# A new hand-written order of steps for a kernel that runs selective scan, layer norms and FFN of three rows at once

## The chip, the cores and the metric

One core of one Trainium2 chip runs the kernel. The metric is device time in microseconds (us), from the first to the last instruction of the slowest (here the only) core, median of the runs. TensorE is called PE, VectorE DVE, ScalarE ACT, GpSimd POOL, and SyncE, which here only issues transfers, SP.

## The reference, cut to what matters

Sixteen rows of 512 tokens x 256 features go through one layer: a selective-scan block (Mamba), a residual and a layer norm, then a gated FFN with two hidden layers, a residual and a layer norm.

```
xx, res = split(x @ in_w.T);  xx = silu(causal_conv4(xx))           # 512 channels
delta_r, B, C = split(xx @ xproj_w.T);  delta = softplus(delta_r @ dt_w.T + dt_b)
h[l] = exp(delta*A) * h[l-1] + delta*B*xx     # 16 states per channel
y = sum_n h*C + xx*D;   y = (y * silu(res)) @ out_w.T
x1 = layernorm(x + y)
h = silu(x1 @ w1 * s1) * (x1 @ w2 * s2);  h = gelu(h @ h1 * s);  h = gelu(h @ h2 * s)
out = layernorm(x1 + h @ w3 * s)
```

## The kernel before

The program works on one row (512 tokens) per iteration, but on several rows at once: in `iteration(i)` the row `scan` = i is scanned, `front` = i+1 is prepared for its scan, `tail` = i-1 is gated, projected, normalised and starts its FFN, and `end` = i-2 finishes its FFN. i runs from -1 to 17. Iteration 0 has no tail, 1 no end; 15 has no front, 16 no scan; so 13 iterations (2 to 14) have all four.

An iteration has 64 steps, s = 0 to 63. All five engines walk through the same steps, each in its own strict order, and wait on semaphores for each other's data. A step is thus no moment in time but a place in each queue. Tables of constants say in which step a piece stands: the name tells the piece, the n-th number the step of its n-th instance. A number over 63 means step s-64 of the next iteration, where the same row is `end`.

The scan of a row is 32 pairs p (16 states x 4 blocks of 128 channels, two blocks a pair). For pair p:
- PE: `b_pair` transposes delta\*B\*u of the pair into PSUM, 8 transposes, called T(p) below. PSUM holds two pairs, so T(p) waits for pair p-2: for DVE's product with C (L800), or for the scan itself where the product is on POOL.
- DVE, step 2p: `scan_pair` (L789). Step 2p+1: `c_pair` (L800), C(p) below, except for the pairs in `POOL_PAIRS`, whose scan writes to `hC` in SBUF and whose product POOL makes (L983).
- ACT makes dA by Exp (`EXP_COUNT` says how many in each step) and dB by Copy with a scale.
- POOL, step 2p+1: a DMA adds the product into y (L991). `hC` has three slots.

Before the change T(p) stands in step 2(p-1), first of that step: T(1) in 0, T(21) in 40, T(31) in 60, and T(0) of the next row in 62.

The FFN matmuls are in 32 halves, h(0) to h(31) (`HALF_AT`, `half_tile`), each of 8 matmuls of 512 columns. Odd halves close an output tile: ACT applies Gelu (`GELU_AT`, L716), POOL splits it in a high and a low part (`SPLIT_AT`, L1028 and L1030), which the next layer needs. Then W(0) to W(3) (`E_W3`, `w3_tile`, 16 matmuls of 256 columns), and on DVE E_SCALE, E_ADD, E_STATS, E_NORM. The first FFN layer is `L1_AT` (PE, ACT Tanh, DVE L905 and L912) with `L1_SPLIT_AT` on POOL.

The tail: RES(c) (`T_RES`, PE) feeds ACT's tanh and DVE's gate (`T_GATE`, L884), POOL multiplies it in (step after), then OUT(t) (`T_OUT`, PE), T_ADD, T_STATS, T_NORM, and X1T (`T_X1T`).

The front: XX(c) (`F_XX`, PE), three conv taps on DVE (L815), tanh, product u (L821); then in step 39 DBL (`F_DBL`, PE L463), which needs all four u; in step 40 (`F_DBL_OUT`) ACT copies its result to `xdbl` (L669); DT(c) (`F_DT`, PE L478) reads xdbl and feeds the softplus: Abs, Relu, Exp on ACT, BASE on POOL (`F_BASE`, L999), PLUS and LOST on DVE (`F_PLUS` L835, `F_LOST` L841), four Ln on ACT in step 52, DELTA (L847) and DELTA_U (L852) on DVE in step 53. BT (`F_BT`, PE) makes the B columns; DU (`F_DU`) transposes delta\*u.

`xdbl` is a part of the tile `out_st`, which also holds the finished output of the row `end` until it is stored. So ACT waits for that store before it writes xdbl:

```
if s == F_DBL_OUT:
    act.wait_ge(pe_dbl, r + 1)
    if end is not None:
        act.wait_ge(out_stored, end * 16 + 16)
    nc.scalar.activation(xdbl, misc_ps[0:DTC + STATES, :], ACT.Copy)
```

The store is issued by SP in step `OUT_AT`. SP's queue is in step order too: before the store come the weight loads into the four-slot `ring` of all earlier steps, and the load that reuses the slot of h(m) stands in the step of h(m) and waits until PE has finished h(m) (`load_weights`, L358).

Of the kernel before, what the change touches and what calls it, by code (L numbers as in the profile page):

```python
# [19 lines left out]
TILES = STATES * DC  # L20
PAIRS = TILES // 2
# [16 lines left out]
QUARTERS = 2 * W3_SLOTS  # L38


T_RES = (0, 4, 5, 8)
T_GATE = (2, 5, 7, 11)
T_OUT = (12, 13, 14, 17)
T_ADD = (15, 18)
T_STATS = (17, 18)
T_NORM = 19
T_X1T = (20, 21)
E_W3 = (10, 11, 13, 14)
E_SCALE = (12, 17)
E_ADD = (14, 19)  # L50
E_STATS = (15, 21)
E_NORM = 22
L1_AT = (22, 23, 24, 25, 26, 27, 28, 29)
L1_SPLIT_AT = (22, 24, 25, 27, 28, 29, 30, 31)
HALF_AT = (31, 32, 34, 35, 36, 38, 40, 41, 42, 43, 45, 46, 47, 48, 49, 50, 51, 52, 53, 54, 55, 57, 59, 60, 62,
           63, 64, 65, 66, 68, 69, 71)
GELU_AT = (38, 39, 39, 46, 46, 47, 50, 51, 55, 57, 57, 65, 66, 67, 71, 71)
SPLIT_AT = (40, 42, 43, 48, 48, 49, 51, 52, 59, 59, 61, 66, 66, 67, 72, 73)
F_XX = (30, 32, 34, 36)
FIRST_XX = (30, 31, 32, 33)  # L60
F_DBL = 39
F_DBL_OUT = 40
F_BT = 46
F_BT_OUT = 51
F_DT = (40, 41, 43, 44)
F_PLUS = (45, 46, 48, 50)
F_BASE = (40, 41, 43, 46)
F_LOST = (46, 49, 51, 52)
F_LN = 52
F_DELTA = (53, 53, 53, 53)  # L70
F_DELTA_U = (53, 53, 53, 53)
F_Y = (55, 55, 58, 63)
F_DU = (54, 55, 56, 58)
F_XR = 51
SCALE_LEAD = 7

EXP_LEAD, DA_RING = 4, 8
EXP_COUNT = (1, 2, 0, 0, 3, 0, 3, 0, 0, 1, 0, 0, 0, 2, 1, 1, 2, 2, 0, 0, 3, 1, 1, 0, 1, 1, 2, 1, 2, 1, 0, 1, 1,  # L80
             0, 1, 1, 2, 2, 1, 0, 2, 1, 0, 1, 2, 2, 0, 0, 2, 2, 0, 0, 0, 2, 2, 2, 0, 0, 1, 1, 0, 1, 1, 2)
EXP_FIRST = EXP_LEAD
EXP_AT = [(EXP_FIRST + sum(EXP_COUNT[:s]), EXP_COUNT[s]) for s in range(TILES)]
PREP_AT = (-30, -27, -25, -24, -20, -12, -7, -5, -3, 2, 5, 12, 16, 17, 18, 20, 23, 26, 30, 33, 38, 39)
# [1 line left out]
FLAG_AT = 48  # L86
DVE_SLOTS = 12
X_FRONT_AT = 22
OUT_AT = 24
X32 = 4  # L90
RAW = 4
HC_SLOTS = 3
POOL_PAIRS = (0, 8, 12, 13, 16, 17)
FIRST_POOL_PAIRS = (0, 3, 4, 9, 14, 16, 17, 18, 25, 27, 28)


# [10 lines left out]
def build(nc, x, xT_in, in_wT, chan, xproj_wT, dt_wT, out_wT, ffn_w, ffn_s, w3_s, ident_in, out):  # L107
# [3 lines left out]
    with ExitStack() as ctx:  # L111
# [172 lines left out]
        def _(sp):  # L284
# [42 lines left out]
            def entry_step(e, full):  # L327

                used = e - (FULL_RING if full else RING)
                if used < 0:  # L330
                    return E_W3[-1]
                if used < FIRST_HALF:
                    return L1_AT[used]
                if used < FIRST_W3:
                    return HALF_AT[used - FIRST_HALF]
                return TILES + E_W3[(used - FIRST_W3) // QUARTERS]

# [77 lines left out]
        def _(pe):  # L415
# [14 lines left out]
            def b_pair(r, p):  # L430
                n, half = divmod(p, 2)
                if half == 0:
                    pe.wait_ge(dB_ready, r * (STATES * TT) + (n + 1) * TT)
                g = r * PAIRS + p - 2
                if g >= 0 and on_pool(g // PAIRS, g % PAIRS):
                    pe.wait_ge(scan_done, g + 1)
                elif g >= 0:
                    wait_product(pe, *divmod(g, PAIRS))
                for k in range(2):
                    c = 2 * half + k  # L440
                    transposes(scan_ps[:, 2 * (p % 2) + k], lambda t: dB[:, n % 2, t, c * P:(c + 1) * P], TT
                               ).then_inc(pe_dBu, 1)
# [46 lines left out]
            def tail_step(r, par, s):  # L489
                if s in T_RES:  # L490
                    c = T_RES.index(s)
                    if c:
# [7 lines left out]
                    in_proj(misc_ps, DC + c, xT_tail).then_inc(pe_res, 1)  # L500
                if s in T_OUT:
                    t = T_OUT.index(s)
                    if t == 0:
# [85 lines left out]
            def iteration(i, par, full):  # L589
                (scan, _), (front, fpar), (tail, tpar), (end, _) = rows(i, par)  # L590
                for s in range(TILES):
                    if s % 2 == 0:
                        if s // 2 + 1 < PAIRS:
                            if scan is not None:
                                b_pair(scan, s // 2 + 1)
                        elif front is not None:
                            b_pair(front, 0)
                    if i == 0 and s == FLAG_AT + 1:
                        pe.wait_ge(low_summed, 1)
                        nc.tensor.matmul(ffn_ps[0][0:1, 0:1], low_sum[:], ones[:], start=True, stop=True  # L600
                                         ).then_inc(low_total, 1)
                    if end is not None and s in E_W3:
                        w3_tile(end, E_W3.index(s), full)
                    if tail is not None:
                        tail_step(tail, tpar, s)
                    if front is not None:
                        front_step(i, front, fpar, s, tail)
                    if end is not None:
                        if s + TILES in HALF_AT:
                            half_tile(end, HALF_AT.index(s + TILES), full)  # L610
                    if tail is not None:
                        if s in L1_AT:
                            l1_tile(tail, L1_AT.index(s), full)
                        if s in HALF_AT:
                            half_tile(tail, HALF_AT.index(s), full)

# [12 lines left out]
        def _(act):  # L629
# [71 lines left out]
            def tail_step(r, s):  # L701
                if s in T_GATE:
                    c = T_GATE.index(s)
                    act.wait_ge(pe_res, r * DC + (c + 1))
# [52 lines left out]
        def _(dve):  # L757
# [216 lines left out]
        def _(pool):  # L974
# [65 lines left out]
            def iteration(i, par):  # L1040
                (scan, spar), (front, fpar), (tail, tpar), (end, _) = rows(i, par)
                for s in range(TILES):
                    if scan is not None and s % 2:
                        y_pair(scan, spar, s // 2)
                    if tail is not None:
                        if s - 1 in T_GATE:
                            gate_tile(tail, tpar, T_GATE.index(s - 1))
                        if s == T_STATS[-1]:
                            rstd_of(0, tail)
                        ffn_step(tail, s)  # L1050
                    if end is not None:
                        if s == E_STATS[-1]:
                            rstd_of(1, end)
# [62 lines left out]
```

## Time and profile before

| | |
|---|---|
| median of 3 runs | 2786.72 us (2784.66 to 2788.4) |
| profiled execution, its own time | 2779.47 us |
| its span | 2777.7 us |
| PE / DVE / ACT / POOL busy | 88% / 87% / 76% / 59% |
| mean granted PE clock | 0.944 |
| DMA | 209 GB/s mean |

Busy time is a share of the span. Idle time "until" a releaser is time in which an engine stood still until the named instruction of another engine had finished; it is printed in brackets behind an instruction, or summed over a window.

### The profile page before, as it was taken

How to read it: one execution, taken by the hardware profiler on the slowest of the kernel's cores; microseconds unless marked ns; L12 is line 12 of the kernel's file. 1: busy time of each engine (PE TensorE's matmuls, PEld its weight loads, DVE VectorE, ACT ScalarE, POOL GpSimd, SP SyncE). 2: the span in 40 equal slices, each digit the busy share in tenths (PEclk: the TensorE clock that was granted, in tenths of full speed). 3: DMA queues.
4: the chain of work that ended last, by engine and by line, in shares of the span. 5: the costliest groups of instructions: out<-in, count | busy, mean ns of one | idle time of the engine just before them, and what ended most of it. 6: DMA issues, size and time to landing. Idle time of an engine off the chain costs nothing. (4 is left out here: it accounts for less than half of the span.)

```text
span 2777.7 us, 36139 instructions
## 1 busy us (share of the span) xinstructions
PE 2439.1 (88%) x12034; PEld 1849.5 (67%) x12034; DVE 2418.8 (87%) x2386; ACT 2117.6 (76%) x3225; POOL 1635.3 (59%) x1577
## 2 busy tenths in 40 slices
PE   4467998989899898989989899998989999898988
PEld 2345676766767676676757677675766767676767
DVE  6789899999999989999998999999898999989730
ACT  5676887969788796978879697887969789696711
POOL 1345656665665666566556656655665675666644
PEclk7568999999999999999999999999999999999999
DMA  5988898989889898998989889898988889898933
GB/s 168 310 201 192 204 225 195 235 198 222 212 206 228 192 237 200 217 215 206 225 191 239 204 214 211 208 223 200 234 209 208 211 209 224 204 229 203 251 98 118
DMA packets 226798, 581.68 MB, mean 209 GB/s; under 512 B 25920, under 2 KB 26304, under 8 KB 226128
## 3 DMA queue, kind: packets, MB, share of 16 engines
q0 software_dynamic: 73728, 268.47, 52.3%
q1 hardware_dynamic: 152880, 310.84, 33.4%
q8 instruction: 99, 1.62, 0.2%
q14 instruction: 91, 0.75, 0.1%
HBM read 301.86 MB, written 20.45 MB: 116 GB/s over the span
## 5 line engine op out<-in xcount | busy, mean ns | idle before, releaser
L789 DVE TENSOR_TENSOR_SCAN scan_ps<-dA,scan_ps 128x1024 f32<-128x1024 f32 x411 | 939.8, 2287 | 121.6 <-PE scan_ps L421 116.5
L991 POOL DMA_DIRECT2D y<-hC x512 | 449.6, 878 | 676.2 <-DVE hC L800 513.7
L648 ACT ACTIVATE dB<-duT,bT 128x512 f32<-128x512 f32 x1024 | 715.4, 711 | 119.5 <-PE scan_ps L421 119.5
L421 PE MATMUL scan_ps<-ident,dB 128*128 128x128 f32 x4096 | 580.4, 288 | 147.5 <-DVE hC L800 121.3
L639 ACT ACTIVATE dA<-delta,a_neg 128x512 f32<-128x512 f32 (+1 forms) x1024 | 692.4, 711 | 1.1
L534 PE MATMUL ffn_ps<-hb_hi,ring 128*128 128x512 f32 x1536 | 652.4, 425 | 35.8 <-POOL hb_lo L1030 20.7
L421 PEld LDWEIGHTS scan_ps<-ident,dB 128*128 128x128 f32 x4096 | 501.6, 148 | 264.2 <-DVE hC L800 100.9
L534 PE MATMUL ffn_ps<-hb_lo,ring 128*128 128x512 f32 x1536 | 609.1, 397 | 0.0
L800 DVE TENSOR_TENSOR hC<-scan_ps,c_rows_sb 128x1024 f32<-128x1024 f32 x411 | 500.6, 1218 | 41.6 <-DMA y<-hC 9.7
L534 PE MATMUL ffn_ps<-ha_hi,ring 128*128 128x512 f32 x1024 | 437.9, 428 | 6.5 <-POOL ha_lo L1030 4.6
L534 PE MATMUL ffn_ps<-ha_lo,ring 128*128 128x512 f32 x1024 | 403.0, 394 | 0.0
L534 PEld LDWEIGHTS ffn_ps<-hb_hi,ring 128*128 128x128 f32 x1536 | 294.4, 192 | 130.3 <-DVE gate L905 36.5
L1030 POOL TENSOR_TENSOR ha_lo<-x,ha_hi 128x512 fp32r<-128x512 f32 x256 | 328.7, 1284 | 21.2
L534 PEld LDWEIGHTS ffn_ps<-hb_lo,ring 128*128 128x128 f32 x1536 | 295.2, 192 | 64.5 <-issue 10.8
L983 POOL TENSOR_TENSOR hC<-hC,c_rows_sb 128x1024 f32<-128x1024 f32 x101 | 253.1, 2506 | 122.4 <-DVE hC L789 120.6
L534 PEld LDWEIGHTS ffn_ps<-ha_hi,ring 128*128 128x128 f32 x1024 | 193.5, 189 | 99.3 <-issue 52.5
L1028 POOL CAST ha_hi<-x 128x512 fp32r<-128x512 f32 x256 | 204.5, 799 | 84.0 <-DVE x L912 69.4
L716 ACT ACTIVATE x<-ffn_ps,fs 128x512 f32<-128x512 f32 x256 | 172.8, 687 | 104.8 <-PE ffn_ps L534 102.6
L789 DVE TENSOR_TENSOR_SCAN hC<-dA,scan_ps 128x1024 f32<-128x1024 f32 x101 | 229.9, 2277 | 13.9 <-DMA y<-hC 10.1
L534 PEld LDWEIGHTS ffn_ps<-ha_lo,ring 128*128 128x128 f32 x1024 | 193.9, 189 | 48.1 <-issue 12.9
L1030 POOL TENSOR_TENSOR hb_lo<-x,hb_hi 128x512 fp32r<-128x512 f32 x128 | 167.9, 1312 | 10.6
L725 ACT ACTIVATE gate<-ffn_ps,s_half 128x512 f32<-128x512 f32 x128 | 88.3, 690 | 103.2 <-PE ffn_ps L534 103.2
(99 smaller groups left out, 3154.5 us busy)
## 6 DMA issues: line engine op xcount, KB each, us to landing
y<-hC POOLq DMA_DIRECT2D x512, 512.0 KB, 5.9
ring<-rounded_weights SPq DMA_DIRECT2D x704, 256.0 KB, 4.1
c_rows_sb<-c_rows SPq DMA_DIRECT2D x256, 256.0 KB, 4.7
x<-ffn_w SPq DMA_DIRECT2D x22, 512.0 KB, 7.7
rounded_weights<-ffn_w SPq DMA_DIRECT2D x22, 512.0 KB, 9.2
xt<-x_chan SPq DMA_DIRECT2D x16, 512.0 KB, 3.8
xt<-x_tok SPq DMA_DIRECT2D x16, 512.0 KB, 4.7
out_st<-x_chan SPq DMA_DIRECT2D x16, 512.0 KB, 4.2
```

Source lines behind the costliest of these rows:

```text
L421: mm = nc.tensor.transpose(dst[:, j * P:(j + 1) * P], src(j), ident[:])
L534: mm = nc.tensor.matmul(dst, w, a, start=(first and n == 0), stop=(last and n == len(steps) - 1))
L639: nc.scalar.activation(dA[:, s % DA_RING, s % 2:], delta2[:, par, c, s % 2:], ACT.Exp, scale=a_neg[:, c, n:n + 1]).then_inc(dA_ready, 1)
L648: nc.scalar.activation(dB[:, n % 2, t, :], duT[:, t, :], ACT.Copy, scale=bT2[:, par, t, n:n + 1]).then_inc(dB_ready, 1)
L716: nc.scalar.activation(x32[:, i % X32, :], ffn_ps[(2 * HC + i) % 3][:], ACT.Gelu, scale=fs[:, 2 + i // HC, i % HC:i % HC + 1]).then_inc(ge ...
L725: nc.scalar.activation(gate[:, o % 2, :], ffn_ps[2 * o % 3][:], ACT.Tanh, scale=s1_half[:, o:o + 1]).then_inc(l1_tanh, 1)
L789: nc.vector.tensor_tensor_scan(states, dA[:, a:a + 2, :].rearrange("p a l -> p (a l)"), b, 0.0, ALU.mult, ALU.add).then_inc(scan_done, 1)
L800: nc.vector.tensor_tensor(hC[:, (r * PAIRS + p) % HC_SLOTS], scan_ps[:, h:h + 2, :], c_rows[:, n % 2].unsqueeze(1).to_broadcast([P, 2, SEQ ...
L983: nc.gpsimd.tensor_tensor(hC[:, slot], hC[:, slot], c_rows[:, n % 2].unsqueeze(1).to_broadcast([P, 2, SEQ]), ALU.mult).then_inc(hC_pool, 1)
L991: pool.dma_start(y2[:, par, c:c + 2, :], hC[:, slot], accum_op=ALU.add).then_inc(y_added[p % 2], 16)
L1028: nc.gpsimd.tensor_copy(hi[:, i % HC, :], x32[:, i % X32, :]).then_inc(ffn_hi, 1)
L1030: nc.gpsimd.tensor_tensor(lo[:, i % HC, :], x32[:, i % X32, :], hi[:, i % HC, :].bitcast(F32), ALU.subtract).then_inc(ffn_lo, 1)
```

## The change

Only the order changes; no instruction is added or removed, and the number of pairs on POOL stays at six of 32.
- T(p) gets a table of its own, `B_AT`. Most of it equals the old rule; T(26) goes from step 50 to 51, T(31) from 60 to 61.
- Halves: h(5) 38 to 37, h(6) 40 to 38, h(7) 41 to 40, h(10) 45 to 44, h(11) 46 to 45, several of h(21) to h(25) one or two steps earlier, h(24) 62 to 61, and the last ones later: h(28) 66 to 67, h(30) 69 to 71, h(31) 71 to 72.
- DT(3) 44 to 45; BT 46 to 48; PLUS from 45, 46, 48, 50 to 43, 44, 47, 49; LOST, BASE and the splits beside them.
- The tail and end pieces of steps 0 to 21 are laid out anew: RES, W, OUT, E_SCALE.
- The store of the output, `OUT_AT`, goes from step 24 to 39.
- POOL's pairs: 0 and 13 are replaced by 2 and 11.

```diff
-T_RES = (0, 4, 5, 8)
-T_GATE = (2, 5, 7, 11)
-T_OUT = (12, 13, 14, 17)
+T_RES = (1, 5, 7, 9)
+T_GATE = (3, 5, 7, 11)
+T_OUT = (13, 14, 16, 17)
-T_STATS = (17, 18)
+T_STATS = (16, 18)
-E_W3 = (10, 11, 13, 14)
-E_SCALE = (12, 17)
-E_ADD = (14, 19)
-E_STATS = (15, 21)
+E_W3 = (11, 12, 15, 16)
+E_SCALE = (14, 18)
+E_ADD = (15, 19)
+E_STATS = (16, 21)
-L1_AT = (22, 23, 24, 25, 26, 27, 28, 29)
-L1_SPLIT_AT = (22, 24, 25, 27, 28, 29, 30, 31)
-HALF_AT = (31, 32, 34, 35, 36, 38, 40, 41, 42, 43, 45, 46, 47, 48, 49, 50, 51, 52, 53, 54, 55, 57, 59, 60, 62,
-           63, 64, 65, 66, 68, 69, 71)
-GELU_AT = (38, 39, 39, 46, 46, 47, 50, 51, 55, 57, 57, 65, 66, 67, 71, 71)
-SPLIT_AT = (40, 42, 43, 48, 48, 49, 51, 52, 59, 59, 61, 66, 66, 67, 72, 73)
+B_AT = (-2, 0, 2, 4, 6, 8, 10, 12, 14, 16, 18, 20, 22, 24, 26, 28, 30, 32, 34, 36, 38, 40, 42, 44, 46, 48, 51, 52,
+        54, 56, 58, 61)
+L1_AT = (22, 23, 25, 26, 27, 28, 29, 31)
+L1_SPLIT_AT = (22, 23, 24, 25, 27, 29, 30, 31)
+HALF_AT = (31, 32, 34, 35, 36, 37, 38, 40, 42, 43, 44, 45, 47, 48, 49, 50, 51, 52, 53, 54, 55, 56, 57, 59, 61, 62,
+           63, 65, 67, 69, 71, 72)
+GELU_AT = (38, 38, 39, 46, 46, 46, 49, 51, 55, 56, 57, 65, 66, 66, 71, 72)
+SPLIT_AT = (39, 41, 42, 47, 47, 49, 51, 51, 59, 60, 61, 65, 66, 68, 71, 71)
-F_BT = 46
-F_BT_OUT = 51
-F_DT = (40, 41, 43, 44)
-F_PLUS = (45, 46, 48, 50)
-F_BASE = (40, 41, 43, 46)
-F_LOST = (46, 49, 51, 52)
+F_BT = 48
+F_BT_OUT = 50
+F_DT = (40, 41, 43, 45)
+F_PLUS = (43, 44, 47, 49)
+F_BASE = (41, 45, 46, 50)
+F_LOST = (44, 47, 51, 53)
-F_Y = (55, 55, 58, 63)
-F_DU = (54, 55, 56, 58)
+F_Y = (56, 58, 58, 63)
+F_DU = (54, 56, 57, 59)
...
-OUT_AT = 24
+OUT_AT = 39
-POOL_PAIRS = (0, 8, 12, 13, 16, 17)
+POOL_PAIRS = (2, 8, 11, 12, 16, 17)
...
                 for s in range(TILES):
-                    if s % 2 == 0:
-                        if s // 2 + 1 < PAIRS:
-                            if scan is not None:
-                                b_pair(scan, s // 2 + 1)
-                        elif front is not None:
-                            b_pair(front, 0)
+                    if scan is not None and s in B_AT:
+                        b_pair(scan, B_AT.index(s))
+                    if front is not None and s - TILES in B_AT:
+                        b_pair(front, B_AT.index(s - TILES))
```

`EXP_COUNT` is rewritten too: the running count of Exp instructions differs from the old one by at most one in any step, and their total is the same.

## Rows read from the trace of the kernel before

**Rows 1.** DVE's DELTA_U groups, first and last of 13 (start us, duration us).
```profile
509.66 2.48 DVE L852 TENSOR_TENSOR du<-y,delta 128x512 f32<-128x512 f32 x4
...
2465.50 2.48 DVE L852 TENSOR_TENSOR du<-y,delta 128x512 f32<-128x512 f32 x4
```

**Rows 2.** Busy time in one period: PE, PEld, DVE, ACT, POOL, PEclk, DMA.
```profile
1327.09:1490.07 162.98, 148.95 (x754) 113.04 (x752) 150.71 (x149) 132.54 (x202) 101.34 (x98) 0.98 0.89 213
```

**Rows 3.** What DVE waited for in that period: us in total, times, longest.
```profile
DVE scan_ps L789 <- PE scan_ps L421: 7.3, 5, 3.4
DVE gate L884 <- ACT gate L707: 2.1, 3, 1.3
DVE delta L847 <- ACT out_st L688: 0.2, 1, 0.2
```

**Rows 4.** DVE timeline: scans 27, 7 (E_ADD behind it), 9.
```profile
1327.09 2.28 DVE L789 TENSOR_TENSOR_SCAN scan_ps<-dA,scan_ps 128x1024 f32<-128x1024 f32 x1
...
1377.16 2.28 DVE L789 TENSOR_TENSOR_SCAN scan_ps<-dA,scan_ps 128x1024 f32<-128x1024 f32 x1
1379.36 0.67 DVE L927 TENSOR_TENSOR out_st<-out_st,x 128x512 f32<-128x512 f32 x1
...
1386.49 2.30 DVE L789 TENSOR_TENSOR_SCAN scan_ps<-dA,scan_ps 128x1024 f32<-128x1024 f32 x1 [0.64 <-PE scan_ps L421]
```

**Rows 5.** DVE timeline: scan 22, C(22), scans 23 and 26, LOST, DELTA, scan 27.
```profile
1459.73 2.29 DVE L789 TENSOR_TENSOR_SCAN scan_ps<-dA,scan_ps 128x1024 f32<-128x1024 f32 x1 [3.41 <-PE scan_ps L421]
1462.15 1.22 DVE L800 TENSOR_TENSOR hC<-scan_ps,c_rows_sb 128x1024 f32<-128x1024 f32 x1
...
1465.52 2.29 DVE L789 TENSOR_TENSOR_SCAN scan_ps<-dA,scan_ps 128x1024 f32<-128x1024 f32 x1 [1.81 <-PE scan_ps L421]
...
1479.93 2.28 DVE L789 TENSOR_TENSOR_SCAN scan_ps<-dA,scan_ps 128x1024 f32<-128x1024 f32 x1
1482.13 1.45 DVE L841 SCALAR_TENSOR_TENSOR delta<-out_st,delta 128x512 f32<-128x512 f32 x1
...
1484.89 1.05 DVE L847 TENSOR_TENSOR delta<-out_st,delta 128x512 f32<-128x512 f32 x1 [0.19 <-ACT out_st L688]
...
1490.07 2.28 DVE L789 TENSOR_TENSOR_SCAN scan_ps<-dA,scan_ps 128x1024 f32<-128x1024 f32 x1
```

**Rows 6.** PE timeline, stretch between two rows' scans: T(0), T(8), T(9).
```profile
1342.49 1.06 PE L421 MATMUL scan_ps<-ident,dB 128*128 128x128 f32 x8 [0.69 <-DVE hC L800]
...
1380.83 1.04 PE L421 MATMUL scan_ps<-ident,dB 128*128 128x128 f32 x8
...
1385.35 1.04 PE L421 MATMUL scan_ps<-ident,dB 128*128 128x128 f32 x8
```

**Rows 7.** PE timeline of the softplus stretch: DBL, T(21), T(25), T(26).
```profile
1447.90 3.63 PE L463 MATMUL misc_ps<-y,xprojw 128*48 128x512 f32 x8 [1.45 <-DVE y L821]
1451.47 1.09 PE L421 MATMUL scan_ps<-ident,dB 128*128 128x128 f32 x8
...
1474.08 1.03 PE L421 MATMUL scan_ps<-ident,dB 128*128 128x128 f32 x8
...
1478.60 1.03 PE L421 MATMUL scan_ps<-ident,dB 128*128 128x128 f32 x8
```

**Rows 8.** ACT timeline: the copy to xdbl.
```profile
1451.57 0.59 ACT L669 ACTIVATE out_st<-misc_ps 48x512 f32<-48x512 f32 x1
```

**Rows 9.** SP timeline: ring load behind h(6), and the output store of that row.
```profile
1408.63 1.14 SPq L381 DMA_DIRECT2D out_tok<-out_st  x1
...
1455.68 0.32 SPq L358 DMA_DIRECT2D ring<-rounded_weights  x1
```

**Rows 10.** All 16 output stores, issue to landing.
```profile
DMA to landing us min/median/max: 2.6/5.0/6.7
```

**Rows 11.** POOL's accumulating transfers, issue to landing (last column, median).
```profile
y<-hC POOLq DMA_DIRECT2D x512, 512.0 KB, 5.9
```

**Rows 12.** POOL timeline: a split beside LOST and DELTA.
```profile
1481.73 1.29 POOL L1030 TENSOR_TENSOR hb_lo<-x,hb_hi 128x512 fp32r<-128x512 f32 x1
...
1484.12 1.27 POOL L1030 TENSOR_TENSOR hb_lo<-x,hb_hi 128x512 fp32r<-128x512 f32 x1
```

More of the change, by code:

```diff
@@ L79 @@
 EXP_LEAD, DA_RING = 4, 8
-EXP_COUNT = (1, 2, 0, 0, 3, 0, 3, 0, 0, 1, 0, 0, 0, 2, 1, 1, 2, 2, 0, 0, 3, 1, 1, 0, 1, 1, 2, 1, 2, 1, 0, 1, 1,
-             0, 1, 1, 2, 2, 1, 0, 2, 1, 0, 1, 2, 2, 0, 0, 2, 2, 0, 0, 0, 2, 2, 2, 0, 0, 1, 1, 0, 1, 1, 2)
+EXP_COUNT = (1, 2, 0, 0, 2, 0, 4, 0, 0, 1, 0, 0, 1, 2, 0, 2, 0, 3, 0, 0, 3, 0, 1, 1, 2, 0, 2, 0, 2, 2, 1, 0, 1, 1,
+             0, 0, 3, 2, 1, 0, 2, 1, 1, 1, 1, 1, 0, 0, 3, 2, 0, 0, 0, 2, 3, 1, 0, 0, 0, 1, 0, 2, 1, 2)
 EXP_FIRST = EXP_LEAD
```

## The prediction

> **What bounds the kernel now.** Start with what repeats. The 13 DELTA_U groups from 509.66 to 2465.50 us are 12 periods of 162.99 us [rows 1]: one row of the batch costs 163 us, and whatever the change does, it does 13 times. Then the busy time in one period: DVE works 150.7 of 162.98 us, PE 149.0 [rows 2]. Two engines are within 2 us of each other, so neither is "the" bound: the reader has to ask of each stretch which of the two is waited for.
>
> The waits of DVE give that. In a period it stands still 7.3 us for transposes, 2.1 us for ACT's gate tanh and 0.2 us for a Ln, together 9.6 us [rows 3]; the rest of its 12.3 idle us are the small gaps between instructions. That 9.6 us is the most an order of steps can win where it adds no gap: 13 x 9.6 = 125 us.
>
> Now the two timelines, side by side. They fall into four legs.
> - Leg 1, from T(0) at 1342.49 to T(9) at 1385.35 [rows 6], is paced by PE: scan 9 starts 0.64 us late on T(9) [rows 4]. DVE's waits of this leg are all of rows 3 except the 3.41 and 1.81 us of scans 22 and 23 and the Ln: 7.3 - 3.41 - 1.81 + 2.1 = 4.2 us [rows 3, 5].
> - Leg 2, from scan 9 at 1386.49 to DBL at 1447.90, is paced by DVE: it has no DVE wait, and PE waits 1.45 us for the last u before DBL [rows 4, 7].
> - Leg 3, from DBL to T(26) at 1478.60, is PE's: 30.7 us without a stop [rows 7], while DVE waits 3.41 and 1.81 us [rows 5].
> - Leg 4, from scan 26 at 1479.93 to C(30) and the next T(0), is DVE's again: T(0) waits 0.69 us for C(30) [rows 5, 6].
>
> The path runs PE, DVE, PE, DVE. A wait inside a PE leg is won only if PE has less to do before the last transpose of that leg.
>
> **The change, leg by leg.**
>
> *Leg 1.* Before, T(0) to T(9) had between them h(24) and all of h(25) to h(31), RES, W(0) to W(3), OUT(0) to OUT(2). After, h(24) stands in front of T(0), and W(3) and OUT(2) behind T(9) (same step, after it). A half costs 1.8 us: T(25) to T(26) is 4.52 us with two halves and a transpose group of some 0.9 [rows 7]. W(3) with OUT(2) is the distance T(8) to T(9), 4.52 less 0.9 = 3.6 us [rows 6]. So PE reaches T(9) up to 5.4 us sooner; DVE needed it 4.2 us sooner at most, and PE stops being the pace. I follow DVE through steps 62 to 20 in the new order and find one wait left, about 0.5 us, for the tanh of gate 1: RES(1) stands behind h(28), T(3). The order also costs something. Where nothing stands between a scan and its own C, C starts 2.42 us after the scan [rows 5]; with a filler in the even step the filler starts after 2.20 [rows 4]. In steps 2 and 12 the fillers (gate 0, E_SCALE 0) go to odd or pool steps, the new pool pair 2 takes one of these gaps away: net about 0.2 us. Leg 1: -4.2 + 0.5 + 0.2 = -3.5 us. What is hidden in front of T(0) is h(24): PE waited 0.69 us there [rows 6], and in front of T(26) to T(29) a split and the DU chain leave it another 1 to 2 us.
>
> *Leg 2.* DVE's instructions are the same; L1 tiles and pool pairs trade places (step 22 loses a gap, 24 gains one). The price of the moves is 0. PE gets l1(7) behind XX(0), so h(1) will wait some 2 us for the last split; XX(2) waits for conv taps anyway, so this is cover that PE's idle time pays. Leg 2: 0.
>
> *Leg 3.* Between DBL and T(26) stood nine halves, h(6) to h(14), four DT and BT. After: h(7) to h(15), four DT and BT, five transpose groups in both. PE's 30.7 us stay. Nearly all waits that scans 22 and 23 lose come back at scans 24 and 26. What does change is the entry. The store of the output now stands in SP's step 39, behind the ring load that waits for the end of h(6) in step 38. h(6) will end just as u is ready, that is when DBL starts. SP then issues the load (0.32 us) and the store, about 0.5 us after h(6) [rows 9]; stores land 5.0 us (2.6 to 6.7) after their issue [rows 10]. ACT may write xdbl 5.5 us after h(6), where before it did so 3.67 us after DBL began [rows 7, 8]. DT(0) reads xdbl, and PE's queue stands behind it. If h(6) ends 0.2 us before DBL, leg 3 grows by 5.5 - 3.67 - 0.2 = 1.6 us; by the extremes of the landing, 0 to 3.3 us. Steady-state stores landed near 5, so I take 1.6. The old place had 43 us of cover (1408.63 to 1451.57) [rows 8, 9].
>
> *Leg 4.* Before, scan 26 to scan 27 took 10.14 us [rows 5]. LOST(3) in it lasted 1.45 us and the first DELTA 1.05, both with a POOL split running [rows 5, 12], where their uncontended kin take 0.68. After, h(15) stands in front of T(26) and both last splits in step 51: POOL is through with them before LOST(3), about 1.1 us. The Ln of three channels no longer stands behind LOST(3), 0.2 us. Scan 26 had 0.2 us of slack to T(26), now none, 0.2. Leg 4: -1.5 us.
>
> The cause of those long instructions is also a rule: the Trainium skill, SBUF — State Buffer, section Who interferes with whom, says that a VectorE instruction with two SBUF inputs, or in a two-port mode, and a GpSimd instruction that reads SBUF exclude each other for their whole length. The trace agrees: 1.45 against 0.68 us.
>
> Sum per full period: -3.5 + 0 + 1.6 - 1.5 = **-3.4 us**, 162.98 to about 159.6. Over 13 periods: -44 us. Iteration 15 has no front but leg 1: -3.5. Iteration 1 has no end, so no leg 1 and no store: about -1. The start (iterations -1, 0) and the end (16, 17, PE alone, same matmuls): 0. Total -48.5. The profiled execution would go from 2779.5 to about 2731; the median of the runs lies 7.2 us above that execution, so 2786.7 - 48.5 = 2738.
>
> **The rivals.**
> - *The store is hidden* (chance 0.18): h(6) ends 2 us before the last u, or the store lands in 3 us. Then a period gains 5.0, the total is 13 x 5.0 + 4.5 = 70: 2717 us. Against it: landings [rows 10].
> - *Half of it lost to new waits* (0.20): T_ADD(1) needs OUT(3), which PE reaches at nearly the same moment; or the store lands after 6.7 us. A period gains 1.2 to 2: 2760 to 2770 us.
> - *The lock moves instead of going* (0.05): by the rule above PLUS, LOST, DELTA, DELTA_U and Y, 20 instructions, can each be caught by a split. A catch costs about 0.75 us [rows 5, 12]; four more of them outside DVE's waits than now take 3 of the 3.4 us. About 2782. For it: BASE and the splits move beside PLUS and LOST; against: in leg 3 DVE waits anyway.
> - *Slower: POOL blocks* (0.13). Split 15 stands in POOL's step 7, its Gelu in ACT's step 8, behind h(31). POOL stands there, behind it gate 2 and the transfers y(4) and y(5). C(7) needs the `hC` slot of y(4), which lands 5.9 us after its issue [rows 11]. By my walk y(4) lands some 1 us before C(7) wants it. If POOL is later by x > 1 us, DVE waits x - 1, and T(9), W(3), OUT(3) with it. From x = 4.4 us on the period is longer than before; at 6 us it is 1.6 us longer: about 2808. Against it: POOL is the idlest of the four [rows 2].
> - The forecast itself: 0.44.
>
> **How the numbers follow.** Less than 0.2% either way (5.6 us) is about what a measurement of this kernel can tell from no change. Faster: 0.44 + 0.18 + 0.20 = 0.82, of which 0.01 is taken for misses; same: the lock rival and the edge of the others, 0.07; slower 0.12. The likeliest case alone spans 2725 to 2752 (store 0 to 3.3 us a period gives the sides). The 8-in-10 range reaches from the hidden store, 2712, to the upper end of the lost half and a little more, 2778.
>
> **What the profile of the changed kernel would show.** Right: periods of 159 to 160 us; no wait of scan 9 on T(9) and less than 1 us on gates; the store issued within 1 us of the end of h(6); ACT's L669 waiting for out_tok and PE idle before DT(0) for 1 to 2 us; LOST(3) at 0.7 us. Wrong: L669 without a wait (hidden store); DVE waiting for y<-hC at C(7) (slower rival); T_ADD(1) waiting for OUT(3); more L841 and L847 above 1 us.

## The result and the profile after

The changed kernel takes 2839.72 us (median of 4 runs, 2823.25 to 2846.12) beside 2786.23 for the one before: ratio 1.0187, 95% interval 1.0151 to 1.0223. I forecast 2738. It is slower by 1.9%, and its runs differ more among themselves than those of before do.

The profiled execution took 2834.73 us, its span is 2832.9. DELTA_U again marks the periods (start, duration), to be held against [rows 1]:

```profile
514.64 2.49 DVE L852 TENSOR_TENSOR du<-y,delta 128x512 f32<-128x512 f32 x4
...
2518.20 2.49 DVE L852 TENSOR_TENSOR du<-y,delta 128x512 f32<-128x512 f32 x4
```

(2518.20 - 514.64) / 12 = 167.0 us a period, before 163.0. All 13 periods together grew by 50.2 us, start and end by 2.5 us each; that is the whole difference of the spans, 55.2. The periods are no longer equal, either: 164.8 to 171.3 us. Two of them, and one more from the middle (length, PE, PEld, DVE, ACT, POOL busy, granted clock, DMA share, GB/s; compare [rows 2]):

```profile
514.64:680.27 165.63, 149.22 (x754) 113.64 (x753) 148.67 (x149) 132.02 (x202) 101.18 (x98) 0.98 0.87 210
...
680.27:849.13 168.86, 154.53 (x754) 117.68 (x753) 149.02 (x149) 131.99 (x202) 100.64 (x98) 0.94 0.86 206
...
1349.43:1516.62 167.19, 152.69 (x754) 117.07 (x753) 149.56 (x149) 131.87 (x202) 100.71 (x98) 0.95 0.87 208
```

DVE's work did not grow; it waits more. The clock of PE, 0.98 before, differs from period to period. It is a mean over two levels, 1.2 and 2.4 GHz (granted 0.5 and 1.0): before, 8.4 us of each period passed at the lower one, in one place, around a stop of PE of 2.8 us; now it is 12.9 us on average, in other places too. DVE's waits over two periods (1352.3 to 1685.5; us, times, longest; [rows 3] are for one):

```profile
DVE scan_ps L789 <- PE scan_ps L423: 13.2, 10, 1.9
DVE gate L884 <- ACT gate L707: 5.5, 6, 1.5
DVE xt L891 <- PE misc_ps L510: 3.7, 2, 1.9
DVE y L815 <- ACT y L656: 2.4, 3, 1.7
DVE xt L891 <- PE ffn_ps L510: 2.4, 2, 1.2
```

The first two groups are those of before: 6.6 instead of 7.3 us a period for transposes, 2.8 instead of 2.1 for gates. The next three are new: T_ADD(0), the conv taps that stand behind XX(2), T_ADD(1). PE's timeline of the first place says why:

```profile
1394.94 0.28 PE L536 MATMUL ffn_ps<-ring,ha_lo 128*128 128x256 f32 x1
1397.71 0.35 PE L536 MATMUL ffn_ps<-ring,ha_hi 128*128 128x256 f32 x1 [2.49 <-DMA ring<-rounded_weights]
...
1398.26 1.89 PE L423 MATMUL scan_ps<-ident,dB 128*128 128x128 f32 x8
```

W(0) stands still for 2.49 us in front of its last quarter, for weights whose load SP issued when h(31) was done:

```profile
1391.24 0.32 SPq L360 DMA_DIRECT2D ring<-rounded_weights  x1
```

It landed 6.3 us later. W(0) itself began 2.3 us after that issue. In the kernel before it began 3.2 us after it, and the load landed after 4.2 us (mean of 13 periods); W(0)'s last quarter, 1.6 us behind its first, had 0.6 us to spare. In the changed kernel the means are 2.3 and 6.3 us. The load and W(0) of before, then W(0) of the changed kernel:

```profile
1366.95 0.32 SPq L358 DMA_DIRECT2D ring<-rounded_weights  x1
```

```profile
1370.14 0.36 PE L534 MATMUL ffn_ps<-ring,ha_hi 128*128 128x256 f32 x1
```

```profile
1393.55 0.36 PE L536 MATMUL ffn_ps<-ring,ha_hi 128*128 128x256 f32 x1
```

So the order takes 0.9 us away, as T(5) now stands in front of h(31) and no longer between h(31) and W(0), and the landing takes 2.1 us longer: 0.9 + 2.1 - 0.6 = 2.4 us, the mean stop. Which transfers lengthen it no run separates in full: POOL's pairs and Exp alone, on another base, make it 4.7 us instead of 4.0 (b_softplus_pairs_exp beside b_new_softplus).

The transposes behind the stop take 1.89 us instead of 1.03 [rows 6, 7]: the clock has fallen. The second place is h(1), which waits for POOL's split of the last tile of the first FFN layer:

```profile
1458.70 0.50 PE L536 MATMUL ffn_ps<-ha_hi,ring 128*128 128x512 f32 x1 [2.14 <-POOL ha_lo L1030]
...
1461.49 1.83 PE L423 MATMUL scan_ps<-ident,dB 128*128 128x128 f32 x8
```

The clock falls again, XX(2) comes late, and DVE waits for its conv base:

```profile
1465.89 2.32 DVE L815 SCALAR_TENSOR_TENSOR y<-misc_ps,conv_half,y 128x511 f32<-128x511 f32 x3 [1.69 <-ACT y L656]
```

Third, the store of the output, with ACT's copy to xdbl and PE's DT(0) behind it, where before ACT wrote xdbl at once [rows 8]. SP, ACT, PE:

```profile
1478.04 0.43 SPq L383 DMA_DIRECT2D out_tok<-out_st  x1
```

```profile
1482.21 0.59 ACT L669 ACTIVATE out_st<-misc_ps 48x512 f32<-48x512 f32 x1 [1.34 <-DMA out_tok<-out_st]
```

```profile
1477.58 3.63 PE L465 MATMUL misc_ps<-y,xprojw 128*48 128x512 f32 x8
1481.14 1.09 PE L423 MATMUL scan_ps<-ident,dB 128*128 128x128 f32 x8
1482.86 1.12 PE L480 MATMUL misc_ps<-out_st,dtw 16*128 16x512 f32 x2 [0.62 <-ACT out_st L669]
```

Fourth, the end of the softplus stretch on DVE, as forecast against [rows 5]: LOST(3) and DELTA at 0.68 us, scan 26 to scan 27 in 8.99 us.

```profile
1510.04 2.29 DVE L789 TENSOR_TENSOR_SCAN scan_ps<-dA,scan_ps 128x1024 f32<-128x1024 f32 x1 [1.59 <-PE scan_ps L423]
...
1513.61 0.68 DVE L841 SCALAR_TENSOR_TENSOR delta<-out_st,delta 128x512 f32<-128x512 f32 x1
1514.21 0.69 DVE L847 TENSOR_TENSOR delta<-out_st,delta 128x512 f32<-128x512 f32 x1
...
1519.03 2.29 DVE L789 TENSOR_TENSOR_SCAN scan_ps<-dA,scan_ps 128x1024 f32<-128x1024 f32 x1
```

The starts of the 32 scans on DVE cut a period into stretches that every run can be compared by. The means over the 13 full periods, in us, worked out from the DVE timelines of the profiled executions, with the median of the runs in the last column:

| run | s27-s0 | s0-s9 | s9-s10 | s10-s15 | s15-s19 | s19-s26 | s26-s27 | period | median |
|---|---|---|---|---|---|---|---|---|---|
| before | 19.82 | 39.59 | 7.07 | 28.95 | 22.46 | 34.92 | 10.17 | 162.98 | 2786 |
| after | 19.52 | 39.36 | 8.92 | 27.98 | 25.11 | 36.97 | 8.99 | 166.84 | 2840 |
| a_h31_early | 19.59 | 38.54 | 7.95 | 27.60 | 25.51 | 36.51 | 8.98 | 164.69 | 2802 |
| a_old_tail_end | 19.54 | 39.66 | 7.06 | 27.75 | 24.88 | 37.78 | 8.99 | 165.66 | 2809 |
| a_old_l1 | 19.58 | 38.90 | 8.92 | 29.35 | 22.47 | 37.31 | 8.98 | 165.51 | 2812 |
| a_out24 | 19.58 | 39.61 | 8.91 | 28.01 | 25.35 | 35.00 | 8.99 | 165.46 | 2818 |
| a_w3_load_cut | 19.58 | 38.01 | 8.68 | 27.85 | 25.06 | 36.61 | 8.99 | 164.78 | 2814 |
| a_w1_load_cut | 19.57 | 39.75 | 8.92 | 27.93 | 24.93 | 36.25 | 8.99 | 166.33 | 2831 |
| a_h31_l1_out24 | 19.57 | 38.29 | 7.78 | 29.52 | 22.55 | 35.00 | 8.99 | 161.70 | 2767 |
| r_h29_behind_res1 | 19.57 | 38.22 | 7.85 | 29.48 | 22.55 | 35.01 | 8.98 | 161.68 | 2768 |
| r_pe_relieved | 19.58 | 36.86 | 8.61 | 29.62 | 22.58 | 35.01 | 8.99 | 161.25 | 2750 |
| r_act_relieved | 19.57 | 38.27 | 7.88 | 29.40 | 22.78 | 35.01 | 8.99 | 161.90 | 2765 |
| r_both_relieved | 19.62 | 36.72 | 8.64 | 29.37 | 22.64 | 35.01 | 8.98 | 160.99 | 2749 |
| b_new_softplus | 19.54 | 39.63 | 7.06 | 29.06 | 22.46 | 35.01 | 8.99 | 161.73 | 2761 |
| b_softplus_out39 | 19.56 | 39.58 | 7.06 | 28.95 | 22.45 | 36.94 | 8.99 | 163.53 | 2792 |
| b_softplus_pairs_exp | 19.56 | 39.72 | 7.06 | 29.19 | 22.50 | 35.01 | 8.99 | 162.01 | 2771 |
| b_softplus_old_b | 19.55 | 39.59 | 7.06 | 28.95 | 22.44 | 33.33 | 9.93 | 160.86 | 2751 |
| b_out39 | 19.81 | 39.68 | 7.06 | 28.95 | 22.45 | 35.29 | 10.19 | 163.43 | 2789 |
| r_old_b_pairs_exp | 19.58 | 38.38 | 7.77 | 28.95 | 22.46 | 33.33 | 9.93 | 160.39 | 2742 |

Leg 1 of the prediction is s0-s9; E_SCALE(1) moved from in front of scan 9 to behind it (0.6 us), so s0-s10 is the fair sum: 46.66 before, 48.28 after. Leg 2 is s10-s19, leg 3 s19-s26, leg 4 s26-s0. Medians carry some 0.2% (the intervals of the ratios are 0.15 to 0.35% to each side); the stretches are steadier, where a run's periods are equal.

### The profile page after: what moved, and what is told of

The parts are those of the page before. It is cut to its first block and busy times, and to the rows that moved or that the text cites. A ratio compares the mean times of both kernels' runs of the same rounds, so it can differ in the third digit from the quotient of the medians.

```text
span 2832.9 us, 36139 instructions
## 1 busy us (share of the span) xinstructions
PE 2469.8 (87%) x12034; PEld 1877.1 (66%) x12034; DVE 2404.5 (85%) x2386; ACT 2109.0 (74%) x3225; POOL 1623.3 (57%) x1577
## 5 line engine op out<-in xcount | busy, mean ns | idle before, releaser
L423 PE MATMUL scan_ps<-ident,dB 128*128 128x128 f32 x4096 | 589.7, 292 | 139.3 <-DVE hC L800 99.5
L536 PE MATMUL ffn_ps<-hb_hi,ring 128*128 128x512 f32 x1536 | 660.6, 430 | 34.3 <-POOL hb_lo L1030 18.4
L423 PEld LDWEIGHTS scan_ps<-ident,dB 128*128 128x128 f32 x4096 | 510.6, 150 | 261.6 <-issue 101.3
L536 PE MATMUL ffn_ps<-ha_lo,ring 128*128 128x512 f32 x1024 | 409.6, 400 | 0.0
L536 PE MATMUL ffn_ps<-ring,ha_hi 128*128 128x256 f32 x512 | 140.0, 308 | 35.9 <-DMA ring<-rounded_weights 33.7
```

The costliest lines, as they stand in the source:

```text
L423: mm = nc.tensor.transpose(dst[:, j * P:(j + 1) * P], src(j), ident[:])
L536: mm = nc.tensor.matmul(dst, w, a, start=(first and n == 0), stop=(last and n == len(steps) - 1))
```

## The experiments

**One piece of the change undone at a time.** First h(31) and its neighbours.

```diff
-HALF_AT = (..., 65, 67, 69, 71, 72)
+HALF_AT = (..., 65, 66, 68, 69, 71)
-GELU_AT = (..., 66, 71, 72)
+GELU_AT = (..., 66, 71, 71)
```

> The changed kernel with the last four FFN halves of a row back in their old steps: h(28), h(30), h(31) in 66, 69, 71 and their Gelus in 71; all else as changed. Theory 'ring': in the changed kernel W(0) waits 2 to 3 us a period for the last quarter of the W3 weights, whose transfer may start only when h(31) is done, and T_ADD(0) and T_ADD(1) on DVE wait 1.9 and 1.2 us for it. Then the wait of W(0) falls under 1 us, the T_ADD waits go, and a period falls by 1 to 2.5 us: 13 to 32 us in all against the changed kernel (2807 to 2827). Rival 'PE has too much to do in this stretch, whatever the order': the wait on the transfer goes, but scans and gates wait for PE instead and the time stays within 6 us.

Measured: 2801.54 us, 38 below the changed kernel, somewhat more than the ring theory asked for. The wait of W(0) is gone (0.2 us in all over 12 periods), s0-s10 falls by 1.8 us. W(0) now begins 4.0 us after the issue of its last load, which lands after 5.3 us.

```diff
-T_RES = (1, 5, 7, 9) ...   # with T_GATE, T_OUT, T_STATS, E_W3, E_SCALE, E_ADD, E_STATS
+T_RES = (0, 4, 5, 8) ...
-HALF_AT = (..., 61, 62, 63, 65, 67, 69, 71, 72)
+HALF_AT = (..., 62, 63, 64, 65, 66, 68, 69, 71)   # Gelus 12 to 15 and their splits too
```

> The changed kernel with steps 62 to 21 of the tail and the end as before: T_RES, T_GATE, T_OUT, T_STATS, E_W3, E_SCALE, E_ADD, E_STATS, h(24) to h(31) and their Gelus and splits. Theory 'the new layout of this stretch is the larger loss': DVE's waits for gates, T_ADD and ring fall from about 5.8 to about 4.2 us or less, a period gets 2 to 3.5 us shorter: 26 to 45 us in all (2795 to 2814). Rival 'the loss sits behind it, in the first FFN layer': at most 10 us.

Measured: 2808.67 us, -31, inside the first theory; s0-s10 is 46.72 us, that of before. But the run above, which keeps the new layout and moves only the last halves, got s0-s10 to 46.49. So the loss of this stretch hangs on the last halves, not on the layout as a whole.

```diff
-L1_AT = (22, 23, 25, 26, 27, 28, 29, 31)
+L1_AT = (22, 23, 24, 25, 26, 27, 28, 29)
-L1_SPLIT_AT = (22, 23, 24, 25, 27, 29, 30, 31)
+L1_SPLIT_AT = (22, 24, 25, 27, 28, 29, 30, 31)
```

> The changed kernel with L1_AT and L1_SPLIT_AT as before (last tile in 29, last split in 31). Theory 'late split': in the changed kernel the last tile of the first FFN layer stands behind C(15) and three conv taps on DVE, its split ends late and h(1) waits 1.5 to 3 us for it on PE, with XX(2) behind it and in some rows at half the clock. Then that wait falls under 0.7 us, DVE no longer waits 2 us for the conv base, and a period gets 1 to 2.5 us shorter: 13 to 32 us in all. Rival 'hidden': PE has to wait for the conv taps anyway (as I held in the prediction), so no change beyond 6 us.

Measured: 2811.64 us, -28. s15-s19 goes from 25.11 to 22.47 us, its old value, and s10-s15 takes 1.4 us back, because the tile stands in it again. "Hidden", which is what I held in leg 2, falls.

```diff
-OUT_AT = 39
+OUT_AT = 24
```

> The changed kernel with the store of the output back in SP's step 24. The changed kernel's ACT waits 1.2 to 2.3 us (once 4.4) for the store before it writes xdbl, and PE stands 0.5 to 1.6 us (once 3.7) before DT(0). Theory of the prediction: a wait on the path; both go, and a period gets 0.6 to 1.5 us shorter: 8 to 20 us in all. Rival: hidden, because DVE waits for its transposes behind it anyway: within 5 us.

Measured: 2818.25 us, -21. s19-s26 falls by 1.97 us. The store's wait lay on the path.

**The transfer by itself.** Two runs cut a load of W3 weights from 512 to 64 columns and leave the order alone.

```diff
+cols = 64 if not full and e == FIRST_W3 + 3 else ENTRY_COLS      # a_w1_load_cut: + 1
-sp.dma_start(dst, src[:, (half % 2) * ENTRY_COLS:(half % 2 + 1) * ENTRY_COLS]
+sp.dma_start(dst[:, :cols], src[:, (half % 2) * ENTRY_COLS:(half % 2) * ENTRY_COLS + cols]
```

> The changed kernel, order untouched, but the transfer of the last quarter of the W3 weights (the one that may start only when h(31) is done) brings 64 of its 512 columns; the rest of that ring slot keeps old values, so the output differs. Theory 'ring': that transfer's landing is the cost that putting h(31) early took away. Then W(0)'s wait of 2 to 3 us falls under 1 us and the time falls by 25 to 40 us, to 2800 to 2815, as with h(31) early. Rival 'the place of h(31) mattered in itself (gates, POOL's split, the PE order)': wait gone, but less than 12 us won.

> Control for the run above: the changed kernel with the same cut of the transfer of the second quarter of the W3 weights, which is free to start three halves earlier; the output differs. The same bytes are saved, but the late transfer stays whole. Theory 'ring': W(0)'s wait stays above 1.5 us and the time within 10 us of the changed kernel's. Rival 'less traffic is what helped': a gain like that of the run above.

Measured: 2813.94 and 2831.14 us, -26 and -9. The late transfer is a cause: with it cut, s0-s10 falls from 48.28 to 46.69 us. In the control W(0) waits as long as before (2.4 us a period), s0-s10 is 48.67, and the -9 us are not clear of the spread of its runs (2821.55 to 2844.01, beside 2823.25 to 2846.12). The wait did not fall under 1 us as expected, but from 2.4 to 1.7 us: an eighth of the bytes still landed late, after 5.6 us instead of 6.3. SP and PE in a_w3_load_cut:

```profile
1373.96 0.32 SPq L361 DMA_DIRECT2D ring<-rounded_weights  x1
```

```profile
1379.66 0.36 PE L537 MATMUL ffn_ps<-ring,ha_hi 128*128 128x256 f32 x1 [1.71 <-DMA ring<-rounded_weights]
```

Behind this stop the clock did not fall. Eight microseconds from the stop on in the changed kernel (2.49 us stop), in this run (1.71 us), and in the changed kernel behind h(1) (2.14 us); the granted clock is the third number from the end:

```profile
1396.00:1404.00 8.00, 6.29 (x35) 6.17 (x36) 7.50 (x6) 6.55 (x12) 3.18 (x4) 0.79 0.90 193
```

```profile
1378.00:1386.00 8.00, 6.34 (x46) 6.09 (x47) 6.86 (x7) 8.00 (x14) 3.91 (x5) 1.00 0.86 179
```

```profile
1458.00:1466.00 8.00, 7.30 (x25) 5.45 (x26) 6.24 (x8) 2.17 (x4) 6.60 (x4) 0.79 0.66 144
```

0.79 is a mean over the two levels, 1.2 GHz for a while and 2.4 for the rest. The periods of one execution can be compared by this:

| 13 periods | clock fell behind W(0): times, stop, s0-s10 | did not fall: times, stop, s0-s10 |
|---|---|---|
| after | 7, 2.04 to 2.73, 48.8 | 5, 2.57 to 3.06, 47.7 |
| a_w3_load_cut | 2, 2.00 and 2.01, 48.3 | 11, 1.31 to 2.66, 46.4 |

(One period of the changed kernel had no stop of W(0): 47.4.) So most of the gain of a_w3_load_cut is the shorter stop, 1.3 us in periods without a fall; that the clock falls in two periods and not in seven gives the rest. A fall costs 1.1 us in the changed kernel: T_ADD(0) waits 1.6 to 1.9 us behind one and 0.6 to 1.1 without. The length of a stop does not decide, for the longest ones had no fall behind them. This is where a good part of the unequal periods comes from; for the spread of the runs it is the likely reason, but not shown.

**Three repairs together.**

> Three repairs of the changed kernel together: h(28), h(30), h(31) and their Gelus early, L1_AT and L1_SPLIT_AT as before, the store in step 24. If the three losses are separate, they add up: 2840 - 38 - 28 - 12 = 2762, below the kernel before by 0.8%, and the period is about 161.5 us. Rival 'they overlap' (one late arrival seen in three places): 2775 or more.

Its edits are those of a_h31_early, a_old_l1 and a_out24. Measured: 2767.30 us, ratio to before 0.9936 (0.9912 to 0.9959). 38 + 28 + 21 = 87 would give 2753; 72 of them came. The losses are nearly separate.

**The change's better half, on top of the kernel before.**

```diff
 (kernel before)
+B_AT, F_BT, F_BT_OUT, F_DT, F_PLUS, F_BASE, F_LOST, F_Y, F_DU of the changed kernel
+h(5) to h(23), Gelus 0 to 10 and splits 0 to 10 of the changed kernel
```

> The kernel before with only the new softplus stretch: B_AT, h(5) to h(23) with Gelus and splits, BT, DT, PLUS, BASE, LOST, Y, DU as changed; the store of the output stays in step 24. Theory of the prediction for this part: leg 4 (scan 26 to scan 27) takes 9.0 instead of 10.14 us, leg 3 stays, so a period of 161.5 to 162 us: 13 to 19 us faster than before (2767 to 2773). Rival: leg 1 is PE's, and a DVE that arrives a microsecond earlier only waits longer for its transposes: within 5 us of before.

Measured: 2761.22 us, -24 against the 2785.4 of its own runs of before; ratio 0.9913 (0.9896 to 0.9930). The period falls by 1.25 us, 16 us in all, as expected; s26-s27 is 8.99. Leg 1 did not eat it.

On this base the other parts were added or taken away, one each.

```diff
-OUT_AT = 24
+OUT_AT = 39
```

> The kernel before with the new softplus stretch (2761), and the store of the output in step 39. In the changed kernel the same move cost 21 us. Theory 'on the path': ACT waits 1.2 to 2.3 us for the store, scan 19 to scan 26 grows from 35.0 to 36.3 to 37.5 us, 15 to 30 us in all (2776 to 2791). Rival: the cost needs the other changes: under 8 us.

```diff
-B_AT = (..., 48, 51, 52, 54, 56, 58, 61)
+B_AT = (..., 48, 50, 52, 54, 56, 58, 60)
```

> The kernel before with the new softplus stretch (2761), but T(26) back in step 50, in front of h(15), and T(31) in 60: the transposes get no steps of their own. Theory: T(26) early frees scan 26 by 1.6 us, but h(15), Gelu and the last split come 0.9 us later, so the lock on LOST and DELTA may come back: scan 19 to scan 27 between 1.6 us shorter and the same; the total 0 to 20 us faster. Rival: h(17) then waits longer for the split and T(28) with it: up to 13 us slower.

```diff
+EXP_COUNT and POOL_PAIRS of the changed kernel
```

> The kernel before with the new softplus stretch (2761), and POOL's pairs and EXP_COUNT as changed: the two parts that no run has tried alone, as one. Theory: they move work by a step and cost or win under 0.5 us a period: within 7 us. Rival: pool pair 2 puts a product of 2.4 us in front of the splits and transfers of steps 5 to 7, and DVE waits for an hC slot or a gate: 10 to 25 us slower.

Measured: 2792.09 (+31), 2750.68 (-10.5) and 2771.32 us (+10). The store costs 1.8 us a period, all of it in s19-s26, and some 4 us more at the end (from the last DELTA_U to the end 316.0 us against 312.0; the changed kernel does not show this, 314.7 us against 316.9 in a_out24). T(26) behind h(15) costs s19-s26 1.7 us and gives s26-s27 0.9 back: the transposes' own steps are a loss. Pairs and Exp, which I had priced at nothing, cost 10 us by the medians and 6.1 by the profiled executions: 3.6 in the 13 full periods (0.3 each), 1.7 behind them, 0.7 in front. Where the other 4 us lie stays open.

And the store alone, in the kernel before:

> The kernel before with one number changed: the store of the output in step 39. There h(5) is the last half in front of DBL, and h(6) stands behind it. SP reaches the store when h(5) is done, about 1.5 us before DBL starts; it lands some 5 us later, when ACT wants to write xdbl. Theory of the prediction: the wait is 0 to 0.7 us and the cost under 9 us. Rival 'the late store costs by its step': 20 us or more, as in the run with the new softplus stretch (31 us).

The edit is the same line. Measured: 2789.47 us, ratio 1.0014 (1.0003 to 1.0024). ACT waited for the store 2.5 us in 12 periods, not in each. The step 39 alone is nearly free; with h(6) in front of DBL it costs 31 us. SP reaches the store when the last half in front of it is done, which is what the prediction said.

**What holds the stretch T(0) to T(9).** With three repairs DVE still waited for gate 1, 2.83 us (DVE, then PE, of a_h31_l1_out24):

```profile
1355.49 0.69 DVE L883 SCALAR_TENSOR_TENSOR gate<-gate,misc_ps 128x512 f32<-128x512 f32 x1 [2.83 <-ACT gate L706]
```

```profile
1350.24 1.03 PE L422 MATMUL scan_ps<-ident,dB 128*128 128x128 f32 x8
...
1352.94 1.88 PE L427 MATMUL misc_ps<-out_st,inw 128*128 128x512 f32 x4
```

Between T(3) and RES(1) PE makes h(29). So:

```diff
-HALF_AT = (..., 65, 66, 68, 69, 71)
+HALF_AT = (..., 65, 67, 69, 70, 71)
```

> The three repairs (old L1 steps, store in 24, last halves early), but h(28) to h(31) in steps 67, 69, 70, 71, so that h(29) stands behind RES(1) instead of in front of it. In the run with the three repairs gate 1 waited 2.8 us every period: PE made T(3), h(29) and only then RES(1). Theory 'order on PE': gate 1's wait falls to the 0.5 us that the prediction named, and a period gets 1 to 2.3 us shorter: 13 to 30 us against the three repairs (2767), 2737 to 2754. Rival: PE has the same work up to T(9), so scans wait instead, within 6 us.

Measured: 2767.83 us, nothing. The wait only split, gate 1 and gate 2:

```profile
1348.35 0.69 DVE L883 SCALAR_TENSOR_TENSOR gate<-gate,misc_ps 128x512 f32<-128x512 f32 x1 [1.47 <-ACT gate L706]
...
1354.16 0.69 DVE L883 SCALAR_TENSOR_TENSOR gate<-gate,misc_ps 128x512 f32<-128x512 f32 x1 [1.56 <-ACT gate L706]
```

Then work was taken away from this run, from PE, from ACT, from both.

```diff
 steps = [(entry(e, full)[:, k * P:(k + 1) * P], a[:, kh * HC // 2 + k, :])
-         for k in range(HC // 2) for a in src]
+         for k in range(HC // 2) for a in src][:4 if m >= 27 else None]        # r_pe_relieved
-nc.scalar.activation(..., ACT.Gelu,
+nc.scalar.activation(..., ACT.Gelu if i < 14 else ACT.Copy,                     # r_act_relieved
```

> The run r_h29_behind_res1 (2768), with only 4 of the 8 matmuls in each of h(27) to h(31); the output differs. This takes 5 x 0.9 = 4.5 us of work from PE between T(1) and T(6), none from any other engine. Theory 'PE is the pace there': gate waits (3.4 us a period) fall under 1.5 us and scan 0 to scan 9 shortens by 1.5 to 3 us: 20 to 40 us in all. Rival 'ACT's queue': gates wait as before, under 8 us.

> The run r_h29_behind_res1 with the last two Gelus of a row (tiles 14 and 15) replaced by Copy; the output differs. This takes two table loads of 1.28 us from ACT between gate 2 and gate 3. Theory 'ACT's queue': gate waits fall by 1 us or more a period, 10 to 20 us in all. Rival 'PE': under 6 us.

> Both of the above together; the output differs. Theory of the prediction (DVE's own work is 3.5 us shorter than the stretch, and nothing else holds it): scan 0 to scan 9 shortens by about 3 us or more, 35 to 45 us in all, and the gate waits are gone. Rival: DVE waits for something not named yet.

Measured: 2749.69 (-18), 2764.78 (-3) and 2748.61 us (-19). The two table loads that the second run spares ACT cost next to nothing: its -3 us are within the spread of the runs, and its period is no shorter. PE's amount of work is not the pace of this stretch either. 4.5 us less of it shortens s0-s9 by 1.4 us, but s9-s10 grows by 0.8: s0-s10 gains 0.6 and the period 0.4, some 6 us in all. In the profiled executions the stretch behind the last full period, where PE works alone with the shortened halves, is 9.5 us shorter.

Gate 1 still waits 1.47 us and T_ADD(1) now 0.84 (r_both_relieved):

```profile
1347.64 0.69 DVE L883 SCALAR_TENSOR_TENSOR gate<-gate,misc_ps 128x512 f32<-128x512 f32 x1 [1.47 <-ACT gate L706]
...
1376.12 0.69 DVE L890 TENSOR_TENSOR xt<-ffn_ps,xt 128x512 f32<-128x512 f32 x1 [0.84 <-PE ffn_ps L509]
```

PE's RES(1) and ACT's queue in front of the tanh of gate 1, in the same run:

```profile
1344.11 1.91 PE L427 MATMUL misc_ps<-out_st,inw 128*128 128x512 f32 x4
```

```profile
1343.28 1.28 ACT L638 ACT_TABLE_LOAD   x1
1344.57 1.33 ACT L638 ACTIVATE dA<-delta,a_neg 128x511 f32<-128x511 f32 x2
1345.81 1.32 ACT L647 ACTIVATE dB<-duT,bT 128x512 f32<-128x512 f32 x2
1347.04 0.57 ACT L706 ACTIVATE gate<-misc_ps 128x512 f32<-128x512 f32 x1
```

RES(1) ends at 1346.02, but ACT works without a gap up to the tanh at 1347.04. About 1.0 of the 1.47 us is thus ACT's queue, with a table load in it that stands behind the Gelus of step 66. The second run left this load where it was, for it took out only the two between gate 2 and gate 3. What gate 1 would gain without the load no run tested.

**Everything that costs taken out, the new layout kept.**

> The run r_h29_behind_res1 (2768) with B_AT, POOL_PAIRS and EXP_COUNT as before. It differs from b_softplus_old_b (2751) only in the new layout of steps 62 to 21. If the losses add up (10 us for the transposes, 10 for pairs and Exp), 2748. Theory of the prediction: the new layout is better than the old by 1 us a period or more, so 2740 or less. Rival: gate 1's 1.5 us and T_ADD(1)'s wait eat it, so within 6 us of 2751.

Its edit is r_h29_behind_res1 with `B_AT`, `POOL_PAIRS` and `EXP_COUNT` as before. Measured: 2742.30 us, ratio 0.9848 (0.9829 to 0.9867), the fastest of all. It differs from b_softplus_old_b only in the layout of steps 62 to 21, which is therefore worth 8 us (0.5 us a period), not the 45 of leg 1 (13 x 3.5).

## Why the prediction was wrong

- **The step that failed is leg 1, "-4.2 + 0.5 + 0.2 = -3.5 us".** s0-s10 went from 46.66 to 48.28, +1.6 us. DVE's waits from scan 0 to scan 10 are 5.6 us a period; they were 4.4, and the sum left 0.5 of them. Three things were wrong in it. First, it followed DVE and PE through the new order and not SP: behind the end of h(31) W(0) begins 2.3 us later instead of 3.2, and the load that waits for h(31) lands after 6.3 us instead of 4.2, so W(0)'s last quarter waits 2.4 us; the cut load and the early h(31) show it (-26, -38 us). The sum had named queues past which the store moves, and forgotten the loads that move with the halves. Second, one wait of 0.5 us was left where gate 1 and gate 3 wait 1.5 and 1.0 us. Third, T_ADD(1) did wait for OUT(3), 1.2 us, which I had as a rival. Even repaired, the leg gains 0.5 us: no scan waits for T(9) any more, but 3.5 us of waits remain, nearly all at gates. "PE stops being the pace" was true of T(9) alone. Against the reading that PE's work paces this leg stands r_pe_relieved, where 4.5 us less of it gave 0.6.
- **Leg 2, "The price of the moves is 0", failed too.** I saw that h(1) would wait some 2 us (1.5 to 2.6) and called it cover. s10-s19 grew by 1.7 us; with the old L1 steps it is 51.8 us (a_old_l1), which gave 28 us back in all. In the seven periods in which the clock did not fall behind h(1) it took 52.4 us on average, so 0.6 was not covered. In the other six it took 53.9: T(18) and XX(2) were late, and DVE waited 1.7 us.
- **Leg 3, +1.6 us from the store: right in mechanism and size.** SP issued it as h(6) ended, it landed some 4 to 5 us later (once 7.1), ACT waited 1.2 to 2.3 us. s19-s26 grew by 2.0 us; 1.8 in b_softplus_out39. One period had a wait of 4.4 us and 171.3 us of length. Not counted were some 4 us at the end of the kernel, which the runs on the kernel before show.
- **Leg 4, -1.5 us, right:** s26-s27 10.17 to 8.99, s27-s0 19.82 to 19.52. LOST and DELTA lost most of their long forms when POOL's splits ended earlier (LOST took 1.3 us or more 27 times of 64 before, twice after); that the lock is the cause is argued from their overlap in the trace, no run tested it alone. What the sum did not see is that T(26) in its old step would have given 1.7 us in leg 3 for 0.9 in leg 4.
- **Pool pairs and Exp, priced at nothing:** +10 us. **Start and end, taken as 0:** +2.5 us each.
- **Of the rivals,** "POOL blocks" did not come: DVE's waits for y<-hC are 3 us in 12 periods. "Half of it lost to new waits" named T_ADD(1) and was the nearest, but its price, 1.4 to 2.2 us a period, was under a third of the 7.3 us between forecast and result. The rival that happened, a weight load late for W, wasn't on the list.

By leg, forecast and measured in us a period: -3.5 and +1.6; 0 and +1.7; +1.6 and +2.0; -1.5 and -1.5. The sum is -3.4 against +3.9 (from the table; rounding makes up the 0.1).

## What to carry to other kernels

When pieces of a hand-ordered schedule move, go through every queue that has waits tied to the moved pieces, the queue of the loads first: a ring load sits behind the work that frees its slot. Count the time between that work and the piece that needs the load, not the steps: here both moved by one step, and the time between them still shrank. The landing time can change with the order, too, so a slack of 0.6 us is none. An idle wait of TensorE is not free cover: where the rows of the trace show a lower granted clock behind such a stop, price it with those slower matmuls. When work is taken away to find the pace, look whether the wait itself went, and whether the time was won where it was expected: of 18 us in r_pe_relieved only 6 were. And a layout of many edits is best tried part by part: here two parts gained (the softplus stretch with the old steps of T 34 us, the new tail 8), five lost (38, 28, 21, 10 and 10), and the whole looked like one bad idea.

## What the runs showed of the hardware

- In the changed kernel PE stopped in front of W(0)'s last quarter in 12 of 13 periods. In or behind seven of these stops (2.04 to 2.73 us) the granted clock fell from 1.0 to 0.5, in which groups of eight transposes took up to 1.89 us instead of 1.03; behind the other five (2.57 to 3.06 us) it did not. Which stops bring a fall no run shows. This agrees in kind with what the Trainium skill, TensorE: Matmul & The Clock Gate, section HAM oscillation — how this bites in real kernels, says: waits between groups of matmuls can put the array back to the slower clock in the midst of a kernel.
- A load of 64 columns a partition, an eighth of the bytes, landed 5.6 us after its issue (mean of a_w3_load_cut), the full one after 6.3 us (changed kernel), and the same full load after 4.2 us in the kernel before and 3.0 in r_pe_relieved. In these runs the size of this transfer set its landing less than what else was under way did.
- A table load of ACT took 1.28 us.
